# Gated cross-attention with a ternary feed-forward: the probabilities' transposes move from TensorE to the SP queue, PV to the end of a slot, and rows are finished in place

## What is computed

```python
q = layernorm(x) @ w_q;  k = ctx @ w_k;  v = ctx @ w_v
attn = softmax(where(tril, q @ k.T / sqrt(512), -inf))
x = x + tanh(g_xattn) * (attn @ v)
h = gelu(layernorm(x) @ ternary(W1).T + b1)
x = x + tanh(g_ffn) * (h @ ternary(W2).T + b2)      # ternary(w): -1, 0, 1 by 0.5 * mean|w|
```

## Time and profile before

| | |
|---|---|
| Median of 3 runs | 1746.44 us (1742.77 to 1746.86) |
| The profiled execution: its own time | 1744.55 us |
| its span, first to last instruction | 1742.7 us |
| mean granted TensorE clock over the span | 0.985 |
| PE busy | 1661.5 us (95%) |
| DVE busy | 914.8 us (52%) |
| ACT busy | 659.8 us (38%) |
| POOL busy | 307.8 us (18%) |
| SP's DMA queue, share of 16 DMA engines | 29.5% |

### The profile page before, as it was taken

How to read it: one execution, slowest core, us unless ns; L and a number is a source line. 1 busy time by engine, 2 the same in 40 slices (tenths; PEclk the granted TensorE clock), 3 DMA queues, 4 the chain that set the end, 5 groups by cost and what they waited for, 6 DMA issues and landing times.

```text
span 1742.7 us, 25225 instructions
## 1 busy us (share of the span) xinstructions
PE 1661.5 (95%) x9024; PEld 854.1 (49%) x9024; DVE 914.8 (52%) x1639; ACT 659.8 (38%) x1032; POOL 307.8 (18%) x341
## 2 busy tenths in 40 slices
PE   3699999999999999888999999999999999999998
PEld 1455655565555565454444444444444444444444
DVE  3666666565666666777544443444444444444432
ACT  1223232333323235332344444444444444444443
POOL 1111111111111111112112221222112211222210
PEclk8799999999999999999999999999999999999999
DMA  5233324343434247463221222122221222112210
GB/s 193 62 79 100 76 68 128 55 121 70 107 73 110 66 121 196 118 170 121 67 60 32 66 66 60 30 66 63 63 66 24 66 66 64 45 47 66 67 37 24
DMA packets 183830, 138.69 MB, mean 80 GB/s; under 512 B 144592, under 2 KB 144592, under 8 KB 182608
## 3 DMA queue, kind: packets, MB, share of 16 engines
q1 hardware_dynamic: 183184, 137.42, 29.5%
q10 hardware_dynamic: 576, 0.27, 0.1%
HBM read 70.53 MB, written 33.55 MB: 60 GB/s over the span
## 4 chain that ended last, share of the span: by engine, by line
PE 68%; issue 13%; DVE 12%; ACT 2%; SPq 2%; DMA 1%; POOL 1%; DVEq 0%; POOLq 0%; ACTq 0%
PE t_ps L835 13%; PE pT_ps L940 12%; PE s_ps L940 12%; PE v_ps L835 11%; PE o_ps L900 6%; PE v_ps L913 5%; PE s_ps L863 4%; PE t_ps L882 4%; DVE v_s L798 2%; DVE cmax L574 2%; DVE w_s L746 1%; DVE pT L653 1%; DVE negmax L662 1%; PE pT_ps L848 1%; DVE xn L614 1%
## 5 line engine op out<-in xcount | busy, mean ns | idle before, releaser
L772 DVE SCALAR_TENSOR_TENSOR v_s<-g,sc,v_s 128x512 f16<-128x512 f32 x256 | 248.1, 969 | 467.1 <-ACT v_s L499 463.7
L940 PE MATMUL pT_ps<-w_s,v_s 128*128 128x512 f16 x1024 | 265.6, 379 | 0.8
L940 PE MATMUL s_ps<-w_s,v_s 128*128 128x512 f16 x1024 | 262.8, 379 | 0.0
L835 PE MATMUL v_ps<-ctx_s,w_s 128*128 128x512 f16 x1024 | 241.9, 379 | 0.9 <-DVE w_s L746 0.9
L835 PE MATMUL t_ps<-ctx_s,w_s 128*128 128x512 f16 x1024 | 241.9, 379 | 0.0
L900 PE MATMUL o_ps<-v_s,pT 128*128 128x512 f16 x864 | 202.2, 386 | 28.5 <-DVE pT L653 28.5
L882 PE MATMUL t_ps<-xnT,a_s 128*128 128x256 f16 x1536 | 182.3, 276 | 24.5 <-ACT a_s L482 20.1
L863 PE MATMUL s_ps<-ctx_s,tT 128*128 128x512 f16 (+3 forms) x1152 | 198.1, 326 | 0.5 <-DVE tT L682 0.4
L913 PE MATMUL v_ps<-wv_s,ctx_s 128*128 128x512 f16 x768 | 178.7, 383 | 10.2 <-DVE ctx_s L546 10.2
L499 ACT ACTIVATE v_s<-g,sc 128x512 f16<-128x512 f32 x256 | 184.7, 721 | 8.3
L882 PEld LDWEIGHTS t_ps<-xnT,a_s 128*128 128x128 f16 x1536 | 151.4, 99 | 49.7 <-issue 26.1
(11 more groups left out here) (94 smaller groups left out, 1375.5 us busy)
## 6 DMA issues: line engine op xcount, KB each, us to landing
x_ring<-in_x SPq DMA_DIRECT2D x64, 256.0 KB, 3.0
raw<-in_ctxT SPq DMA_DIRECT2D x8, 2048.0 KB, 7.8
out_y<-x_ring SPq DMA_DIRECT2D x64, 256.0 KB, 3.2
raw<-out_y SPq DMA_DIRECT2D x64, 256.0 KB, 3.3
out_y<-v_s SPq DMA_DIRECT2D x64, 256.0 KB, 2.1
w_in<-in_w1T SPq DMA_DIRECT2D x16, 512.0 KB, 4.4
w_in<-in_w2T SPq DMA_DIRECT2D x16, 512.0 KB, 4.7
xnT<-xn_s SPq DMA_TRANSPOSE x128, 3.3
```

The costliest lines, as they stand in the source:

```text
L772: v.scalar_tensor_tensor(out=g_s[:, f % 4, LO], in0=g32[:, f % 2], scalar=col(C_SG), in1=g_s[:, f % 4, HI], op0=ALU.mult, op1=ALU.subtract ...
L835: last_mm = mm(h_ps[f % 2], w1_s[:, c, (f % FC) * P:(f % FC + 1) * P], yT[:, (f // FC) % 2, a, c, :], start=(a == HI and c == 0), stop=(a ...
L940: last_mm = mm(y_ps[i], g_s[:, f % 4, a, i * P:(i + 1) * P], w2_s[:, f, :], start=(f == 0 and a == HI), stop=(f == FC - 1 and a == LO))
```

## The change

1. TensorE's transposes, the PSUM tile `pT_ps`, DVE's copy of it and the identity matrix are gone. SP issues two DMA transposes per tile instead (`turn_p`), of i + 1 blocks each, once `p_split` says that the probabilities are there. `p_s` and `pT` have two buffers.
2. On TensorE a slot is now S, T, V, PV: PV of tile t-1 comes last.
3. The scaled sum of a tile is written in place into `x_ring`, and `x2_ring` is gone. SP loads tile t+6 in slot t (before: t+7), ahead of `turn_p`, and waits for the store of tile t-2 for it.
4. In SP's slot the weights are loaded behind `turn_p`.

The diff, cut:

```diff
-        p_s = sb("p_s", [P, 2, S], F16)
-        pT = sb("pT", [P, 2, S], F16)
-        x2_ring = sb("x2_ring", [P, 4, D])
+        p_s = sb("p_s", [P, 2, 2, S], F16)
+        pT = sb("pT", [P, 2, 2, TB, P], F16)
...
+            def turn_p(it, s):
+
+                r, w = s % 2, s % TB + 1
+                sp.wait_ge(p_split, it * BODY + s + 1)
+                sp.sem_inc(p_turn_issued, 1)
+                sp.wait_ge(pv_mm, it * BODY + s - 1 + PV0)
+                sp.sem_inc(p_turn_issued, 1)
+                for a in (HI, LO):
+                    sp.dma_start_transpose(pT[:, r, a, 0:w], p_s[:, r, a, 0:w * P]).then_inc(p_turned[r], 16)
+
             def slot(it, s, last=False):
                 t = it * BODY + s
                 if not last or t + XT_LEAD < NT + GT:
                     turn_row(it, s, last)
+                if not last or t + 6 < NT:
+
+                    sp.wait_ge(x2_stored[(s + 6) % 8], it * (BODY // 8) * 16 + ((s - 2) // 8 + 2) * 16)
+                    sp.dma_start(x_ring[:, (s + 6) % 8], x_tiles[t + 6]).then_inc(x_in[(s + 6) % 8], 16)
+                if not last or t < NT:
+                    turn_p(it, s)
                 if last:
                     for m, (at, _, _) in enumerate(W_STEPS):
                         if at == t:
                             load_weights(m)
-                if not last or t + 7 < NT:
-
-                    sp.wait_ge(o_done, t)
-                    sp.dma_start(x_ring[:, (s + 7) % 8], x_tiles[t + 7]).then_inc(x_in[(s + 7) % 8], 16)
                 sp.wait_ge(o_done, t)
-                sp.dma_start(out_tiles[t - 1], x2_ring[:, (s - 1) % 4]).then_inc(x2_stored[(s - 1) % 4], 16)
+                sp.dma_start(out_tiles[t - 1], x_ring[:, (s - 1) % 8]).then_inc(x2_stored[(s - 1) % 8], 16)
...
@@ ScalarE, softmax
-                act.wait_ge(p_tr, t)
-                a.activation(p_s[:, HI, 0:w], p32[:, 0:w], ACT.Copy, scale=P_UP).then_inc(p_hi, 1)
+                act.wait_ge(p_turned[r], p_turned_by(it, s) - 32)
+                a.activation(p_s[:, r, HI, 0:w], p32[:, 0:w], ACT.Copy, scale=P_UP).then_inc(p_hi, 1)
...
@@ VectorE, slot
-                if s >= 1:
-
-                    w = ((s - 1) % TB + 1) * P
-                    dve.wait_ge(p_tr, t)
-                    v.tensor_copy(pT[:, :, 0:w], pT_ps[:, :, 0:w]).then_inc(pT_ready, 1)
...
-                    dve.wait_ge(pv_mm, t)
-
-                    dve.wait_ge(x2_stored[(s - 1) % 4], it * (BODY // 4) * 16 + ((s - 1) // 4 + 1) * 16)
-                    v.scalar_tensor_tensor(out=x2_ring[:, (s - 1) % 4], in0=o_ps[:, :], scalar=osc[:, q:q + 1],
+                    dve.wait_ge(pv_mm, t + PV0)
+                    v.scalar_tensor_tensor(out=x_ring[:, (s - 1) % 8], in0=o_ps[:, :], scalar=osc[:, q:q + 1],
                                            in1=x_ring[:, (s - 1) % 8], op0=ALU.mult, op1=ALU.add).then_inc(o_done, 1)
...
@@ TensorE, slot
-                if s >= 1:
-
-                    pe.wait_ge(p_split, t)
-                    for a in (HI, LO):
-                        for j in range((s - 1) % TB + 1):
-                            tr = nc.tensor.transpose(pT_ps[:, a, j * P:(j + 1) * P], p_s[:, a, j * P:(j + 1) * P],
-                                                     ident[:, :])
-                    tr.then_inc(p_tr, 1)
...
+                if s >= 1:
+
+                    pe.wait_ge(p_turned[(s - 1) % 2], p_turned_by(it, s - 1))
+                    pe.wait_ge(v_split, t + 1 if not last or t < NT else NT)
+                    if last and t == NT:
+                        pe.wait_ge(o_done, NT - 1)
```

More of the change, by code:

```diff
@@ L149, in gated_block @@
         p_exp, p_hi, p_split = sem("p_exp"), sem("p_hi"), sem("p_split")
-        p_tr, pT_ready = sem("p_tr"), sem("pT_ready")
+        p_turned = [sem(f"p_turned{i}") for i in range(2)]
+        p_turn_issued = sem("p_turn_issued")
         pv_mm, o_inv, o_scaled, o_done = sem("pv_mm"), sem("o_inv"), sem("o_scaled"), sem("o_done")
-        x2_stored = [sem(f"x2_stored{i}") for i in range(4)]
+        x2_stored = [sem(f"x2_stored{i}") for i in range(8)]
         w_loaded = [sem(f"w_loaded{i}") for i in range(WR)]
@@ L203, in w_dst, with p_turned_by @@
             return dst[:, :, :].rearrange("p a n -> p (a n)")[:, k * WCH:(k + 1) * WCH]
+        PV0 = 2
+        def p_turned_by(it, s):
+            return it * (BODY // 2) * 32 + (s // 2 + 2) * 32
         def turned_before(it, s):
@@ L226, in _ @@
             sp.dma_start(raw[:, :], ctx_batches[0].rearrange("p c s -> p (c s)")).then_inc(ctx_in, 16)
-            for t in range(3, 8):
+            for t in range(3, 7):
                 load_x(t)
@@ L272, in slot @@
                             load_weights(m)
-                if not last or t + 7 < NT:
-                    sp.wait_ge(o_done, t)
-                    sp.dma_start(x_ring[:, (s + 7) % 8], x_tiles[t + 7]).then_inc(x_in[(s + 7) % 8], 16)
                 sp.wait_ge(o_done, t)
-                sp.dma_start(out_tiles[t - 1], x2_ring[:, (s - 1) % 4]).then_inc(x2_stored[(s - 1) % 4], 16)
+                sp.dma_start(out_tiles[t - 1], x_ring[:, (s - 1) % 8]).then_inc(x2_stored[(s - 1) % 8], 16)
                 if s % TB == 7 and (not last or t + 9 < NT):
                     load_ctx(it * 2 + s // TB + 2)
+            for i in range(8):
+                sp.sem_inc(x2_stored[i], 16)
             for i in range(4):
-                sp.sem_inc(x2_stored[i], 16)
                 sp.sem_inc(y_stored[i], 16)
+            for r in range(2):
+                sp.sem_inc(p_turned[r], 32)
+            sp.sem_inc(pv_mm, PV0)
             sp.sem_inc(y_done, GT)
@@ L288, in _ @@
                 turn_row(0, s)
+            turn_p(0, 0)
             load_ctx(1)
@@ L300, in _ @@
                         load_x2(i, i)
-            for i in range(4):
-                sp.wait_ge(x2_stored[i], 16 * (NT // 4 + 1))
+            for i in range(8):
+                sp.wait_ge(x2_stored[i], 16 * (NT // 8 + 1))
             def group(it, gg, last=False):
@@ L331, in _ @@
             g = nc.gpsimd
-            g.memset(ident[:, :], 0.0).then_inc(consts, 1)
             g.memset(causal[:, :], 0.0).then_inc(consts, 1)
             g.memset(minus_half[:, :], -0.5).then_inc(consts, 1)
-            pool.wait_ge(consts, 3)
-            g.affine_select(out=ident[:, :], in_=ident[:, :], compare_op=ALU.not_equal, fill=1.0, base=0,
-                            pattern=[[-1, P]], channel_multiplier=1).then_inc(consts, 1)
+            pool.wait_ge(consts, 2)
             g.affine_select(out=causal[:, :], in_=causal[:, :], compare_op=ALU.is_ge, fill=NEG, base=0,
@@ L586, in scale_product @@
             def scale_product():
-                for n, half in enumerate((s_ps[:, :], pT32)):
+                for n, half in enumerate((s_ps[:, :], e_ps[:, :])):
                     dve.wait_ge(a_mm, n + 1)
@@ L656, in slot @@
                 if live:
+                    if s == 0:
+                        dve.wait_ge(consts, 3)
                     dve.wait_ge(s_mm, t + 1)
@@ L675, in slot @@
                     dve.wait_ge(p_hi, t + 1)
-                    v.scalar_tensor_tensor(out=p_s[:, LO, 0:(i + 1) * P], in0=p32[:, 0:(i + 1) * P], scalar=P_UP,
-                                           in1=p_s[:, HI, 0:(i + 1) * P], op0=ALU.mult,
+                    v.scalar_tensor_tensor(out=p_s[:, r, LO, 0:(i + 1) * P], in0=p32[:, 0:(i + 1) * P], scalar=P_UP,
+                                           in1=p_s[:, r, HI, 0:(i + 1) * P], op0=ALU.mult,
                                            op1=ALU.subtract).then_inc(p_split, 1)
@@ L889, in slot @@
                     hidden(1, 1, 0)
[L890 to L902, removed]
                 if s >= -1 and (not last or t + 1 < NT):
@@ L915, in slot @@
                     last_mm.then_inc(v_mm, 1)
+                if s >= 1:
[3 more added lines that the diff above has]
+                        pe.wait_ge(o_done, NT - 1)
+                    jn, par = (s - 1) % TB, ((s - 1) // TB) % 2
+                    for n, (pa, va) in enumerate(PASSES):
+                        for j in range(jn + 1):
+                            last_mm = mm(o_ps[:, :], pT[:, (s - 1) % 2, pa, j], v_s[:, par, va, j],
+                                         start=(n == 0 and j == 0), stop=(n == 2 and j == jn))
+                    last_mm.then_inc(pv_mm, 1)
             for s in range(FIRST_SLOT, 1):
```

8 lines of the change are left out of this document (2 added, 6 removed).

## The result

| us | before | after |
|---|---|---|
| Median of 4 runs | 1745.11 (1742.77 to 1746.86) | **1775.55** (1774.36 to 1779.27) |
| Ratio after / before | | **1.018**, 95% interval 1.016 to 1.020 |
| The profiled execution: its own time | 1744.55 | 1774.80 |
| its span | 1742.7 | 1773.0 |
| mean granted TensorE clock | 0.985 | 0.970 |

The change makes the kernel 1.8% slower, though PE is busy 10 us less and DVE 51 us less. (The work taken off PE is more than 10 us: a lower granted clock in the last slots makes PE's busy time longer.

The account below looks back on a forecast made before the run. TensorE was taken to bound steady batches, with VectorE nearly the bound in the last stretch. The terms -30 + 48 + 3 + 3 gave +24 us on 1744.6, so 1769 us, with a range of 1740 to 1800.

Parts of the forecast that it names:

- steady batches, slots 1 to 48: TensorE over six batches: each gains 4.0 us from transposes and 1.1 from the shorter wait, -30 us in all.
- slots 49 to 52: Late chunks for ACT's sums delay exponentials of tiles 50 to 52, mostly hidden by POOL's chain: +3 us, between 0 and 8.
- mask 53 to first hidden product: Last slots: DVE always waits for weights' loads behind the transposes; 193.7 us against 145.5, +48 us.
- clock in the feed-forward: After TensorE stands still over 10 us, the first 6 or 7 us of feed-forward run at clock 0.50: +3 us.
- The closed loop: Slots from 53: next `p_split` waits through DVE, ACT, SP and DMA; 176.3 us for ten slots, mask to mask.
- I take 0.63 per block: SP's issue of a transpose pair grows with blocks, 0.63 us each: 5.1 us at 8 blocks, 30.9 for 49.
- so PE waits 0.4 at V instead of 1.5 at PV: Steady batch, V of slot 5: POOL's late chain costs TensorE less than before, a gain of 1.1 us per batch.
- The rival "the clock": Last slots: waits for V keep the clock at 0.50, PE's 114 us becoming 228; up to 1820 us; 5%.
- The transposes arrive: Steady batches: DMA transposes land before PV needs them, at zero cost, with about 2.5 us cover at tile 7.
- The wait vanishes: Last stretch: the load wait stays below 4 us in VectorE's idle time, the stage keeps its length; 1718 us; 10%.
- Half of both: Landing 3.9 us, pair's issue fixed at 2.5, stage +31, gain 5.5 per batch; 1740 to 1749 us; 10%.
- The transposes are late: A block costs SP twice as much; tile 7's PV waits 2.5 us in 8 places; 1820 us or more; 5%.

Follow-up runs that it names:

- run 1: The changed kernel with the weights' loads issued ahead of the row load and `turn_p` again; 1718.22 us, 0.983 of the kernel before.
- run 2: The kernel before with SP waiting for `p_split` of the slot's own tile ahead of the weights' loads, TensorE still transposing; 1770.42 us, ratio 1.013.
- run 5: The kernel before with POOL's all-reduce of the context's maximum replaced by a plain add, work left out; 1727.22 us, ratio 0.988.
- run 6: run 1 with POOL's all-reduce of the context's maximum replaced by a plain add, work left out; 1700.99 us, 0.973 of the kernel before.
- run 10: run 1 once more, unchanged, as a yardstick; 1722.32 us, 0.986 of the kernel before.
- run 7: The changed kernel with one DMA transpose of twice the blocks per tile in place of the pair; 1762.32 us, 1.008 of the kernel before.
- run 4: run 1 with PV moved back between T and V on TensorE; 1719.12 us, 0.984 of the kernel before.
- run 3: The kernel before with only PV moved last in TensorE's slot, transposes staying on TensorE; 1746.08 us, ratio 1.000.

## Why the prediction came out as it did

The sign, the mechanism of the loss and the size held: +24 us forecast on the profiled execution's time, +30 measured, 1769 against 1775.55 in the runs. Term by term:

| term, us | predicted | measured |
|---|---|---|
| steady batches, slots 1 to 48 | -30 | -20.9 |
| slots 49 to 52 | +3 (0 to 8) | +9.1 |
| mask 53 to first hidden product | +48 | +39.4 |
| clock in the feed-forward | +3 | +2.7 |
| sum | +24 | +30.3 |

Three terms were mis-sized by 6 to 9 us each, and they partly cancel: that the sum is off by only 6 us is in part luck.

**The closed loop: right.** It was predicted as issue, landing, ternary, mask, `p_split`, with the order on SP as the cause; runs 1 and 2 show that cause by taking it away and by putting it in alone. Its parts over the ten slots, as in the table under run 2:

| part, us | predicted | measured |
|---|---|---|
| mask to end of `p_split` instruction | 40.4 | 39.8 |
| from there to the first ternary instruction | 30.9 + 47 = 77.9 | 71.7 |
| from there to the next mask | 30 + 23 + 5 = 58 | 59.1 |
| sum | 176.3 | 170.6 |

The part that was off is the middle one: "I take 0.63 per block", which for 49 blocks is 30.9 us. The other bound in the text, a fixed 2.5 us for a pair, was the true one: 10 x 2.5 + 47 = 72.0. (Over the nine slots without slot 53, which is told of below, the bound gives 64.8 and 62.6 was measured.) These two rows are pairs of 8 blocks and of 1 block in after's timeline:

```profile
429.08 2.61 SPq L277 DMA_TRANSPOSE pT<-p_s  x2
```

```profile
440.86 2.42 SPq L277 DMA_TRANSPOSE pT<-p_s  x2
```

The reason given for the choice, descriptors made block by block, had no row behind it; the 4-block row fits both bounds. Tile 63's end, with its 8 blocks, shrank for the same reason, 14.3 us against 17.4. One slot did not follow the loop: in slot 53 it took 9.1 us from `p_split` to the ternary instruction, but DVE was waiting 7.7 us for POOL's `rstd` behind an all-reduce. Most of the wait for the load is hidden there: before, the same part of slot 53 already took 7.7 us.

**The steady batches: "so PE waits 0.4 at V instead of 1.5 at PV" failed.** The 4.0 us per batch for the transposes fit what was measured (below). But the wait did not shrink. PE in slots 5 and 6 of after, and at the next turn of the loop:

```profile
397.61 2.75 PE L905 MATMUL v_ps<-wv_s,ctx_s 128*128 128x512 f16 x12 [0.77 <-DVE v_s L719]
400.20 3.40 PE L917 MATMUL o_ps<-v_s,pT 128*128 128x512 f16 x15
404.31 4.71 PE L868 MATMUL s_ps<-ctx_s,tT 128*128 128x512 f16 x24 [0.71 <-DVE tT L697]
...
447.01 2.74 PE L868 MATMUL s_ps<-ctx_s,tT 128*128 128x256 f16 x12 [2.91 <-issue]
```

I followed the POOL chain to V of slot 5 (0.77 us, close to the 0.4) and not beyond it. DVE is late by the same chain, so the lower half of T (L697) is late as well, and S of slot 6 waits another 0.71. Together that is 1.5 us, what PV had waited before. PE's waits in the steady batches (166 to 620 us), before and after (total, times, longest):

```profile
PE o_ps L900 <- DVE pT L653: 7.2, 5, 1.6
PE pT_ps L848 <- issue: 3.6, 2, 1.9
```

```profile
PE s_ps L868 <- issue: 5.5, 2, 2.9
PE v_ps L905 <- DVE v_s L719: 3.8, 5, 0.9
PE s_ps L868 <- DVE tT L697: 3.5, 5, 0.7
```

7.2 us in five batches before, 3.8 + 3.5 = 7.3 after. Runs 5 and 6 show the cause: without the all-reduce all of these waits are gone. The second loss is at the loop's turn, every 16 slots, where PE stands with nothing to wait for: 1.8 us each before, 2.75 after. The prediction had no such term. The batch that it added up holds one of these stands, 1.69 us, which is more than all of its "1.1 left over":

```profile
461.99 0.28 PE L848 MATMUL pT_ps<-ident,p_s 128*128 128x128 f16 x2 [1.69 <-issue]
```

Behind the turn of after shown above, S of 2 blocks took 2.74 us; before, in the earlier trace rows's pace of 0.65 us a block, it would take 1.3. The window over that turn shows a granted clock below full (0.72):

```profile
444.00:450.00 6.00, 3.09 (x16) 2.13 (x16) 2.25 (x4) 0.00 (x0) 0.00 (x0) 0.72 1.13 137
```

So a batch gains 4.0, less 0.4 for the turn (1.9 us over 5 batches), less some 0.3 for the clock behind one turn: 3.3, the measured 3.26; six batches of it are 20 us of the 30 forecast. The last two of these terms are smaller than the scatter of single profiles: the same steady code took 91.64, 92.40 and 91.94 us per batch in after and runs 1 and 10, and 94.90 and 95.90 in before and run 2. The means, 92.0 and 95.4, are 3.4 apart, so a gain of some 3.3 stands. How the rest of the 4.0 is split is only argued, and the 4.0 itself is worked out from the row of ten transposes; no run isolates it. (The three batches of this stretch without a turn gained 3.5 us on average, 94.5 to 91.0, the two with one 2.9.) Taken together, the prediction's "1.1 from the wait" is zero and 0.7 was not in it.

**Slots 49 to 52: mis-sized.** "2, 2 and 6 us late, most of it hidden by the POOL chain": the lateness was right in kind, the cover was not. ACT in slot 50 of after, and the exponential of tile 51 behind it:

```profile
653.71 1.06 ACT L465 ACTIVATE w_s<-w_in 128x1024 f16<-128x1024 f32 x1 [4.42 <-DMA w_in<-in_w1T]
...
656.94 1.06 ACT L465 ACTIVATE w_s<-w_in 128x1024 f16<-128x1024 f32 x1 [0.79 <-DMA w_in<-in_w1T]
657.90 0.19 ACT L465 ACTIVATION_READ_ACCUMULATOR w_s<-w_in 128x1 f32 x1
658.00 0.76 ACT L455 ACTIVATE p<-s_ps,ebias,esc 128x512 f32<-128x512 f32 x1
```

The exponential starts right behind the last sum, as forecast. What I had taken for fixed was the POOL chain itself. The all-reduce of slot 51 in after and in before:

```profile
673.44 0.89 POOL L382 PARTITION_ALL_REDUCE call<-cmax  x1 [10.26 <-issue]
```

```profile
683.86 0.68 POOL L364 PARTITION_ALL_REDUCE call<-cmax  x1 [6.01 <-issue]
```

POOL stood 10.3 us in front of it instead of 6.0, and in those 10 us SP issued three chunks (from 662.96) with a turned row behind them. The same wait was 8.9 us in run 2 and 8.7 in run 7, where the chunks are late too, and 6.2 in run 1, where they are not. Over mask 49 to 53 these runs lose 4.0, 5.6 and 0 us against before, and after 9.1. So some 4 of the 9.1 us come from POOL's longer stand; that the chunks' traffic causes it fits all five profiles, but no run moved the traffic alone.

**The clock: right.** Before the first hidden product PE stood still for 8.9 us, and the granted clock in the first stretch of the feed-forward was below full, 0.71, where the kernel before, after a wait of 0.9 us, had 1.00 (first row before, second after):

```profile
843.15:853.40 10.25, 10.25 (x48) 4.61 (x48) 3.75 (x9) 2.82 (x4) 0.00 (x0) 1.00 0.07 26
```

```profile
870.76:881.00 10.24, 10.24 (x34) 4.07 (x35) 1.26 (x5) 2.82 (x4) 0.00 (x0) 0.71 0.08 27
```

What is missing from full clock in these 10.24 us is 0.29 of them, 3.0 us. In the last slots it fell to 0.50 (1.2 GHz) in ten pieces of about 3 to 7 us, behind waits of PE, and was back at 2.4 GHz between them, as in these windows of slots 53 and 54:

```profile
690.00:692.00 2.00, 2.00 (x11) 0.88 (x9) 0.95 (x2) 0.00 (x0) 0.57 (x1) 1.00 0.15 31
...
705.00:707.00 2.00, 2.00 (x6) 0.73 (x5) 1.97 (x4) 0.00 (x0) 0.00 (x0) 0.50 0.59 121
```

The mean of the stretch is 0.87. PE had 52 us to spare there and no wait of DVE in that stretch is for PE, so this cost nothing that the waits show, but it made PE's busy time look larger: 132.5 us, where run 1 has 121.0 for the same work. The rival "the clock" did not happen.

**The transposes arrive: right, with more cover than thought.** PV never waited for them in after; in run 4, which has less cover, 0.4 us once. By the Trainium skill (VectorE: DVE Perf Modes, "The three transpose paths"), taken at 1309 ns for each 128x128, an estimate gives 21 us for tile 7's pair, and PV would wait at every tile 7. The trace disagrees: 16 blocks are issued in 2.6 us and landed at a median of 2.7 us per instruction. The page's figure is near what one instruction costs to issue here, and should not be multiplied by blocks. (The rule to use TensorE, which the prediction cites beside it, stands in the same page's section "Rules for kernel authors".)

**The rivals.** "The wait vanishes" needed a landing under 3 us; it was 4.6 (median). "Half of both" had the pair's price right, but supposed a landing of 3.9 us and a gain of 5.5 per batch, where 4.6 and 3.3 were measured. "The transposes are late" had issue at twice 0.63 us per block, which is 72 us over the last 11 tiles; at 2.5 us a pair it was 28.

## What to carry to other kernels

SP's DMA queue issued in program order in every run here (in slot 62 of after the pair's issue ends at 846.59 and the chunks' begins at 846.65): before adding a wait to such a queue, list what is issued behind that wait, and ask who needs it in the same round. If the wait is on the engine that consumes those loads, a loop closes over both and its whole length becomes the pace; here one block of four lines, moved ahead of the wait, turned 1.8% slower than before into 1.4 to 1.7% faster. And where a long chain is late in a pipeline, follow it through every consumer of the engine that it delays, not only to the first: its lateness is paid in pieces.

## What had not been expected of the hardware

- The issue of a DMA transpose on SP takes about 1.2 to 1.3 us for 1 to 8 blocks of 128x128 (median 1.24 in after) and grows beyond 8: medians of 1.34, 1.44, 1.54 and 1.79 us for 10, 12, 14 and 16 blocks in run 7. From issue to landing it took 2.7 us (median) with up to 8 blocks and 3.5 with up to 16.
- An all-reduce over partitions on POOL (0.4 us in the record) stands between 5.9 us of idle of POOL ahead of it and 7.2 behind it, for which the profile shows no cause, and seven of them are worth 20 us of the kernel before (run 5). The Trainium skill (GPSIMD Engine Reference, "Instruction dispatch") has about 6 us for the first call after code is loaded, and the 5.9 agrees in size; whether code is loaded in front of these calls, no run here shows. Beside late chunks the time ahead grew to 8.7 to 10.3. After's POOL timeline, slot 3:

```profile
386.86 0.37 POOL L382 PARTITION_ALL_REDUCE call<-cmax  x1 [5.89 <-issue]
394.42 0.59 POOL L366 TENSOR_TENSOR rstd<-var_s,minus_half 128x1 f32<-128x1 f32 x1 [7.20 <-issue]
```

- PE's stand at the loop's turn is 1.8 us on average before, 3.2 in run 3, 2.75 in after and 2.9 in run 1. Why it depends on what ends the slot was not tried.
